# Seam from attention to MLP: mean square, norm and weight splits placed one gate tile earlier, waits for the last hs2 store replaced

## The reference

```python
y    = cond(x)                                        # clip(...)
h    = rms_norm(y) * norm_w
gate = gelu(h @ fc_gate_w.T + b)
hs   = h @ fc_w.T + b;  r = sigmoid(h @ fc_r_w.T + b);  i = sigmoid(h @ fc_i_w.T + b)
a    = exp(-8 * softplus(alpha) * r);  s = sqrt(1 - a*a) * hs * i
out  = scan over the tokens: o = a_t * o + s_t
hs2  = out * gate + y                                 # end of "attention"
h2   = rms_norm(hs2) * norm2_w                        # start of "MLP"
g2   = gelu(h2 @ mlp_gate_w.T + b);  f2 = h2 @ mlp_fc_w.T + b
x1   = x + (f2 * g2) @ out_w.T + out_b + hs2
out  = x1 + ffn(conditioned layers of x1)
```

## Time and profile before

| | us |
|---|---|
| median of 3 runs | 1934.48 |
| lowest and highest of them | 1933.43, 1939.89 |
| profiled execution, its own time | 1938.59 |
| its span in the trace | 1936.6 |
| TensorE busy in the span | 1848.2 (95%) |
| VectorE, ScalarE, GpSimd busy | 1010.1, 764.2, 379.8 |

### The profile page before, as it was taken

How to read it: one execution, slowest core, us unless ns; L and a number is a source line. 1 busy time by engine, 2 the same in 40 slices (tenths; PEclk the granted TensorE clock), 3 DMA queues, 4 the chain that set the end, 5 groups by cost and what they waited for, 6 DMA issues and landing times.

```text
span 1936.6 us, 23534 instructions
## 1 busy us (share of the span) xinstructions
PE 1848.2 (95%) x8366; PEld 1489.7 (77%) x8374; DVE 1010.1 (52%) x1641; ACT 764.2 (39%) x1154; POOL 379.8 (20%) x334
## 2 busy tenths in 40 slices
PE   7999999999899999999999999997899999999995
PEld 6788888887788888888888888776677778778773
DVE  6656665657532333233323333357676486586664
ACT  7554655455521222222222122233354455454342
POOL 0111112122000000000000000033164364364331
PEclk9999999999899999999999999998899999999996
DMA  5011111005301010101010102434112122122211
GB/s 187 1 44 44 43 43 44 23 15 183 107 1 66 1 66 0 67 1 65 1 67 0 66 1 87 142 118 140 34 59 82 55 77 88 55 77 88 65 38 39
DMA packets 55760, 115.10 MB, mean 59 GB/s; under 512 B 4290, under 2 KB 4546, under 8 KB 55668
## 3 DMA queue, kind: packets, MB, share of 16 engines
q1 hardware_dynamic: 50532, 96.05, 14.2%
q0 software_dynamic: 4608, 16.78, 2.7%
q10 hardware_dynamic: 528, 1.05, 0.2%
HBM read 88.70 MB, written 25.17 MB: 59 GB/s over the span
## 4 chain that ended last, share of the span: by engine, by line
PE 84%; DVE 5%; issue 3%; DMA 3%; ACT 1%; POOL 1%; DVEq 0%; ACTq 0%; SPq 0%; POOLq 0%
PE bank L802 26%; PE bank L281 17%; PE bank L817 14%; PE bank L1417 10%; PE bank L1453 5%; PE bank L1434 4%; PE bank L267 3%; DMA x_tiles<-x_d 2%; PE bank L1365 1%; DVE operand_parts L1890 1%; DVE operand_full L1880 1%; PE bank L1381 1%; DVE stats L1850 1%; PE bank L831 1%; PE bank L1374 1%
## 5 line engine op out<-in xcount | busy, mean ns | idle before, releaser
L281 PE MATMUL bank<-h_parts,gate_w 128*128 128x512 f32 x1536 | 355.6, 392 | 0.1
L281 PEld LDWEIGHTS bank<-h_parts,gate_w 128*128 128x128 f32 x1536 | 289.1, 188 | 64.6 <-issue 4.9
L1011 DVE SCALAR_TENSOR_TENSOR product_full<-bank,vec_sb,gelu 128x512 f32<-128x512 f32 x96 | 72.0, 750 | 434.9 <-PE bank L802 375.3
L817 PE MATMUL bank<-mlp_out_w,product_parts 128*128 128x512 f32 x1152 | 286.2, 397 | 10.0 <-DVE product_parts L1014 10.0
L1417 PE MATMUL bank<-operand_parts,int_w 128*128 128x512 f32 x1152 | 288.5, 396 | 6.8 <-DVE operand_parts L1890 6.4
L802 PE MATMUL bank<-h_parts,mlp_gate_w 128*128 128x512 f32 x1152 | 276.9, 389 | 1.0 <-DVE h_parts L996 1.0
L802 PE MATMUL bank<-h_parts,mlp_fc_w 128*128 128x512 f32 x1152 | 276.8, 389 | 0.0
L817 PEld LDWEIGHTS bank<-mlp_out_w,product_parts 128*128 128x128 f32 x1152 | 215.6, 189 | 62.7 <-issue 17.1
L1417 PEld LDWEIGHTS bank<-operand_parts,int_w 128*128 128x128 f32 x1152 | 217.0, 190 | 54.0 <-issue 7.0
L802 PEld LDWEIGHTS bank<-h_parts,mlp_gate_w 128*128 128x128 f32 x1152 | 216.2, 188 | 46.6 <-issue 1.8
L802 PEld LDWEIGHTS bank<-h_parts,mlp_fc_w 128*128 128x128 f32 x1152 | 216.3, 188 | 44.9
(11 more groups left out here) (246 smaller groups left out, 2279.2 us busy)
## 6 DMA issues: line engine op xcount, KB each, us to landing
xin<-xT SPq DMA_DIRECT2D x8, 1024.0 KB, 7.0
hs_d<-u SPq DMA_DIRECT2D x8, 1024.0 KB, 5.1
x_tiles<-x SPq DMA_DIRECT2D x8, 1024.0 KB, 5.5
x_d<-x_tiles SPq DMA_DIRECT2D x8, 1024.0 KB, 4.5
x_tiles<-x_d SPq DMA_DIRECT2D x8, 1024.0 KB, 7.3
x_residual<-x_d SPq DMA_DIRECT2D x32, 256.0 KB, 3.4
out<-u_tiles SPq DMA_DIRECT2D x32, 256.0 KB, 2.0
raw_w<-int_W SPq DMA_DIRECT2D x7, 1024.0 KB, 8.0
```

What stands on the lines that cost most here:

```text
L281: i = pe.matmul(bank[:], gw[:, w, s, k, m * P:(m + 1) * P], hr[:, q, t, k, :], start=k == 0 and n == 0, stop=k == KT - 1 and n == 2)
L817: i = pe.matmul(A[t][:], pr[:, j % 2, s, t * P:(t + 1) * P], ow[j // KT][:, w, j % KT, :], start=j == 0 and n == 0, stop=j == FT - 1 and n ...
L1011: dve.scalar_tensor_tensor(out=pf[:], in0=FB[j % 2][:], scalar=v("mlp_fc_b", j), in1=gg[:], op0=ALU.add, op1=ALU.mult).then_inc(p_full, 1)
```

## The change

- TensorE does the mean square of MLP block 0 before gate tile 2 of the last attention block, not before gate tile 3.
- ScalarE splits chunk 0 right after the four squares, behind gate tile 0 (before: behind tile 1); takes the root and splits chunk 1 behind tile 1 (before 2); makes the high part of h2 behind tile 2 (before 3); and splits chunk 2 between the four square roots and the four gelus (before: after the last hs2 tile was added).
- VectorE adds the squares behind tile 0 (before 1), splits chunk 0 and normalises behind tile 1 (before 1 and 2), and splits chunk 1 and makes the low part of h2 behind tile 2 (before 2 and 3).
- `first()` of ScalarE waits for VectorE's last og product and no longer for the last addition and store; that of VectorE has no wait for the store any more.
- TensorE's first two fc products in the MLP also wait for the last two u tiles of VectorE (L569), whose PSUM banks they take.

No instruction is added or removed apart from waits, and SyncE's program is unchanged.

```diff
@@ tensor, attention body @@
                 for m in range(1, KT):
-                    if not nxt and m == 3:
+                    if not nxt and m == 2:
                         early()
                     gates(b, q, m)
@@ scalar, attention body @@
                                    bias=quarter).then_inc(q_done, 1)
+                if not nxt:
+                    early(4)
                 for m in range(KT):
                     act.wait_ge(g_ps, KT * b + m + 1)
@@ tensor, MLP body @@
+                if not prev and j < 2:
+                    pe.wait_ge(att["u"], KT * NB - 1 + j)
@@ scalar, MLP @@
             if m == 0:
                 act.wait_ge(att["projected"], KT * NB)
                 squares(0, 0)
+                split_high(0)
             elif m == 1:
-                split_high(0)
-            elif m == 2:
                 root(0)
                 split_high(1)
-            elif m == 3:
+            elif m == 2:
                 h_parts(0)
+            elif m == 4:
+                split_high(2)
 
         def first():
-            act.wait_ge(att["added"], KT * NB)
-            split_high(2)
-            act.wait_ge(att["stored"], 16 * NB)
+            act.wait_ge(att["product"], KT * NB)
@@ vector, MLP @@
         def early(m):
-            if m == 1:
+            if m == 0:
                 add_squares(0)
+            elif m == 1:
                 split_low(0)
+                normalise(0, 0)
             elif m == 2:
-                normalise(0, 0)
                 split_low(1)
-            elif m == 3:
                 h_low_part(0)
 
         def first():
             split_low(2)
-            dve.wait_ge(att["stored"], 16 * NB)
```

More of the change, by code:

```diff
@@ L203, in attention_half @@
         mlp = following(sems, {"projected": y_ps, "h_high": h_high, "h_low": h_low, "hs": hs_ps, "r": r_ps, "i": i_ps,
-                               "gates": g_ps, "added": hs2_done, "stored": hs2_stored, "gelu": g_evac})
+                               "gates": g_ps, "added": hs2_done, "stored": hs2_stored, "gelu": g_evac,
+                               "product": og_done, "u": u_done})
         @block.sync
```

## The result

The change makes the kernel 0.24% faster: median 1931.9 us of 11 runs (1929.0 to 1935.3) against 1936.9 of 11 runs of the kernel before (1933.4 to 1939.9), ratio 0.9976 with a 95% interval of 0.9968 to 0.9984, so 4.6 us (3.1 to 6.2; the two medians themselves lie 5.0 us apart). I had forecast 7.6 us and 1926.9, with a range of 1924.0 to 1931.5. The direction is right, the size is not. Of the 5.0 us between the forecast 1926.9 and the measured 1931.9, 2.4 us are the starting point: the three runs I had started from had a median of 1934.5, eleven have 1936.9. The other 2.6 us are gain that did not come; the trace shows 2.1 of them at the seam.

A forecast was written before the change was run, and what follows sets the result against it. TensorE, busy 95% of the span, bounds the kernel; a better seam can give 12.67 us. Less 3.4 (stall) and 1.7 (clock) this is 7.6 us, from the three-run median 1934.48 to 1926.9 us; range 1924.0 to 1931.5.

The forecast's parts named there:

- What the change takes away: Chain to the MLP's first output product: GpSimd's additions and the store, 482.99 to about 488.1, leave it.
- The stall at the mean square: TensorE before gate tile 2 of last attention block: stands 3.4 us, up to 4.1, until the mean square starts at 445.6.
- The clock behind it: TensorE behind the mean square's stall: the clock falls, costing 1.7 us, bounds 0 and about 5.
- TensorE ready for the output product: TensorE at the seam: MLP starts at 475.4, four products later, at 486.2, it can start the first output product.
- VectorE's scans: VectorE in the last attention block: scans start at 470.2, 1.0 us sooner than before, bounds 469.6 and 471.3.
- The split of chunk 2 beside the additions: VectorE behind the og products: 2.50 us undisturbed, 0 to 3.2 more beside GpSimd's additions, 1.6 taken; done at 483.7.
- Og products and the last chain: VectorE at the seam: og products end 4.67 us after scans; first MLP product to output product takes 2.40 us.
- The sum: At the seam: output product may start at 486.1, TensorE comes at 486.2, no gap left; gain 7.6 us.
- rival 2: VectorE's chain to the output product is late, part of the gap stays: gain 1.3 to 5.8, 1928.7 to 1933.2; chance 0.22.
- Rival 4: VectorE's split of chunk 2 held until GpSimd's additions end: output product 2.4 us late, gain 5.2, 1929.3 to 1931.8; chance 0.05.
- - 3.4 - 1.7: TensorE's stall at the mean square and its low clock, in us, subtracted from the 12.67 a better seam can give.

The follow-up runs named there:

- e2: Changed kernel with the old waits and chunk 2's high part behind the addition again, only the early steps kept; ratio 0.9997 to the kernel before.
- e1: Changed kernel with mean square and early steps back at their old places, only dropped waits and chunk 2's early split kept; ratio 0.9976 to the kernel before.
- e4: Changed kernel with VectorE's out bias of MLP block 0 added behind MLP tile 2, not in the norm; ratio 0.9953 to the kernel before.
- e8: e7 with the mean square ahead of gate tile 2, where the change put it; ratio 0.9948 to the kernel before.
- e5: Changed kernel with GpSimd's last four additions started only when VectorE has split chunk 2; ratio 0.9950 to the kernel before.
- e3: Changed kernel with the mean square between the r and i products of gate tile 2; ratio 0.9981 to the kernel before.
- e6: Changed kernel with the edits of e3 and e5 together; ratio 0.9956 to the kernel before.
- e7: Changed kernel: mean square between r and i products, out bias later, first MLP product ahead of chunk 2's split, additions behind first low part; ratios 0.9954, 0.9931.

## Why the prediction was right or wrong, point by point

Times of the changed kernel are given less 0.76 us, to stand beside those of the prediction, except where it says "in the trace".

- **What the change takes away**: right. ScalarE's first MLP gelu starts right behind the og products (482.05 in the trace, they end at 482.01) and no store stands in the chain; e2 shows that without this part there is no gain. The early steps of the title, the other part, added nothing that the timed runs can tell (e1).
- **The stall at the mean square**: forecast 3.4 us, start 445.6. Measured 3.03 us of idle, start 446.11 - 0.76 = 445.35. The three adds took 2.0 us as taken.
- **The clock behind it**: forecast 1.7 us. From the mean square to the MLP's start it took 475.90 - 446.11 = 29.79 us (in the trace), at full clock 0.90 + 120 x 0.2267 = 28.10: 1.7 us.
- **TensorE ready for the output product**: forecast 486.2, measured 475.90 + 10.88 - 0.76 = 486.0.
- **VectorE's scans**: forecast 470.2 with bounds 469.6 and 471.3; measured 471.86. **This is the step that failed.** It took over the 22.9 us of work between tile 1 and the scans from before, without asking who works beside it in the new order. In the old order one square of GpSimd fell on the adds and one on the low part of h2, and one on nothing. In the new one they fall on two splits (2.7 to 3.5 us each) and on the products with the decay (2.49 to 3.34): three times 0.8, less the 0.86 that the low part of h2 no longer loses. That is about 1.6 of the 1.7 us. The lengths are read from rows in which the same instructions stand once beside a square and once alone (e1 has the old lengths, every run with the new order the new ones; e4 and e8 part the third pair); that moving the squares would bring the whole 1.6 us back was not tested.
- **The split of chunk 2 beside the additions**: forecast 4.1 us (2.5 + 1.6), bounds 2.5 and 5.7; measured 4.68. e5 shows the cause: 2.49 with the additions out of the way. I had taken two instructions at 0.79 us more each; it was two at 1.10 (1.78 us against 0.68), the other two ran when the additions were over (484.87 in the trace). The Trainium skill, page "SBUF — State Buffer", section "Who interferes with whom", which the prediction weighed, states that a VectorE instruction with two SBUF inputs contends with a GpSimd instruction that reads SBUF. The trace agrees for the split too: 4.68 us beside the additions against 2.50, and 3.52 beside a square against 2.73. I had weighed this for one split only, and not for the two splits and the products that the squares of GpSimd now meet.
- **Og products and the last chain**: 4.66 and 2.39 us against 4.67 and 2.40 forecast.
- **The sum**: output product forecast 486.1, measured 488.17: a gap of 2.15 us where I had none. 7.6 - 2.15 and 0.1 for the rest is the 5.54 measured. Of the 2.1 us by which the output product is later than 486.1, 1.7 are the late scans and 0.6 the third split, less 0.2 in between. That is rival 2 (the chain is late and part of the gap stays, 1.8 to 3.8 us, gain 1.3 to 5.8), at its mild end and with the clock kept; I had given it 0.22. Its effect is the one measured, its reasons only in part: I had named the root, the reciprocal and two splits in a row, or additions that block all four instructions of chunk 2's split. VectorE has no wait for the root here, the squares beside its work are not in my list, and the additions held two instructions of the four. Rival 4's numbers (2.4 us of gap, gain 5.2) lie as near, but not for its reason: it held the whole split until the additions end, while the measured one started at 481.94 and had two of its instructions nearly through when they ended at 484.87 (both in the trace), and it has nothing on the scans.
- **What was wrong beneath the sum**: the terms "- 3.4 - 1.7" are what TensorE loses only if TensorE is later than VectorE at the output product. The right form is the later of two arrivals, TensorE at 486.0 and VectorE at 488.2. As VectorE is later, the stall was free (e3), and by these arrivals it would have been with 2.2 us more. My two arrivals stood 0.1 us apart, so the sum came out as if the stall were the price of the change, and hid that every us by which VectorE is late counts fully.
- **The range**: its upper end was 1931.5, the measurement 1931.9. The median of three runs that it started from was 2.4 us under that of eleven; I had allowed one us for that at the lower end and nothing at the upper. Moved up by these 2.4 us, the forecast would have been 1929.3 and the upper end 1933.9, which holds the measurement; the gain itself would still have been 2.6 to 3.0 us too large (7.6 against 5.0 and 4.6), of which the trace puts 2.1 on VectorE's chain.

## What to carry to other kernels

Where two engines meet, write both arrival times down and take the later; do not subtract what one of them loses, and test it by removing the stall alone. When work is moved along a queue, its duration is not carried along: look at what the other engines do beside it at the new place (here GpSimd's squares, 0.8 us for each that met a split or the products). And a stall that lies in front of a gap is free until the gap closes: then it becomes the bound, as e5 and e8 show.

## What the runs showed of the hardware

One instruction of VectorE's split (scalar_tensor_tensor with both tensors in SBUF) takes 0.68 to 0.75 us alone; four of them took 2.49 to 2.74 us alone, 3.5 beside one square of GpSimd (one of the four took 1.53), 4.6 to 4.8 beside its additions in the change and e1 to e6 but for e2, and 5.85 in e7, where the additions start 0.16 us behind it and last 6.84 us. GpSimd is slowed as well: the square takes 1.04 us alone and 1.48 beside a split.

The granted clock of TensorE went to half (1.2 GHz) behind a single wait of 3.03 us, for 3.4 us, in the change, and stayed full in its gap of 1.98 us that followed full work, as in e7's of 1.31; in e6 a wait of 3.92 us left the whole next product at half clock. Over the 2.72 us of a product at full clock, the one behind a gap took 2.53 us more after 3.92 (e6), 5.71 (e2), 6.17 (e1) and 9.97 us (before), and 2.16 more after 6.78 (e3). Behind the stall of the change the clock cost 1.7 us, behind its gap of 1.98 us 0.1.
